# The tail of a fused attention and feed-forward block in another order

## The reference

```python
x = x + attention(layernorm(x))      # 16 heads of 128, rotary q and k, causal window of 128
x = x + ffn(layernorm(x))            # 256 -> 1024 -> 256

# attention: softmax(where(valid, q k^T / sqrt(128), min)) v, heads joined, times wo
# ffn:
w1q, w2q = ternary(w1), ternary(w2)  # round(w / mean|w|) clipped to -1, 0, 1
h = gelu(x @ w1q.T + b1)             # exact gelu
y = h @ w2q.T + b2
```

## Time and profile before

| | us |
|---|---|
| median of 3 runs | 354.56 |
| lowest and highest | 353.38, 354.79 |
| the profiled execution | 352.97 |
| its span, from first to last instruction | 351.2 |
| PE busy | 337.4 (96%) |
| DVE busy | 271.0 (77%) |
| POOL busy | 223.8 (64%) |
| ACT busy | 205.6 (59%) |

### The profile page before, as it was taken

The page is one execution under the profiler, slowest core; times in us unless marked ns, Lnnn a source line. Parts: engine busy times, 40 slices in busy tenths (PEclk is TensorE's granted clock), DMA queues, the critical chain, the costliest instruction groups (busy, mean ns, idle before and its releaser), DMA issues.

```text
span 351.2 us, 6925 instructions
## 1 busy us (share of the span) xinstructions
PE 337.4 (96%) x2410; PEld 312.5 (89%) x2410; DVE 271.0 (77%) x607; ACT 205.6 (59%) x626; POOL 223.8 (64%) x182
## 2 busy tenths in 40 slices
PE   6987999999999999999999999999999999999896
PEld 6876879999999999999999999999999999878886
DVE  4885886778777887799889887887778777868581
ACT  2335775776775556655665566556665566375180
POOL 2327888767677668889898877777777566411300
PEclk9999999999999999999999999999999999999999
DMA  6935565543333333333333333333322231000001
GB/s 206 242 89 153 146 180 152 125 103 87 82 83 88 90 91 90 92 89 82 77 87 83 86 82 83 89 91 91 90 63 60 63 90 32 0 3 0 32 30 60
DMA packets 29025, 31.25 MB, mean 89 GB/s; under 512 B 3392, under 2 KB 20288, under 8 KB 28992
## 3 DMA queue, kind: packets, MB, share of 16 engines
q1 hardware_dynamic: 28992, 30.82, 34.3%
HBM read 12.98 MB, written 1.05 MB: 40 GB/s over the span
## 4 chain that ended last, share of the span: by engine, by line
PE 81%; DVE 8%; DMA 4%; POOL 2%; ACT 2%; issue 1%; SPq 0%; DVEq 0%; POOLq 0%
PE PR L393 23%; PE OT L472 13%; PE VO L410 12%; PE SC L445 11%; PE VO L427 10%; PE PT L456 4%; DMA swapped<-by_sin 3%; PE PR L500 2%; PE SC L500 2%; PE VO L519 1%; POOL turn L970 1%; DVE stats L708 1%; PE SC L519 1%; DVE gT_lo L825 1%; DVE xnorm L721 1%
## 5 line engine op out<-in xcount | busy, mean ns | idle before, releaser
L975 POOL TENSOR_TENSOR gT_lo<-turn,gT_hi 128x512 fp32r<-128x512 f32 x62 | 82.0, 1323 | 45.7 <-ACT gT_hi L605 45.4
L970 POOL TENSOR_TENSOR turn<-turn,swapped 128x512 f32<-128x512 f32 x62 | 80.2, 1293 | 24.9 <-DMA swapped<-by_sin 24.8
L610 ACT ACTIVATE probs<-SC,negmax 128x128 f32<-128x128 f32 x128 | 45.8, 363 | 75.5 <-DVE negmax L772 75.5
L783 DVE TENSOR_TENSOR probsT<-PT,mask_sb 128x512 f32<-128x512 f32 x64 | 44.1, 690 | 40.4 <-PE PT L456 40.3
L472 PE MATMUL OT<-probsT,v_sb 128*128 128x128 f32 x450 | 60.2, 276 | 1.3 <-DVE gT_lo L790 1.3
L472 PEld LDWEIGHTS OT<-probsT,v_sb 128*128 128x128 f32 x450 | 55.2, 192 | 2.3 <-DVE probsT L783 2.1
L617 ACT ACTIVATE probs<-probs,rinv 128x128 f32<-128x128 f32 x128 | 44.5, 394 | 19.1 <-DVE rinv L777 19.1
L393 PE MATMUL PR<-xT_hi,qk_lo 128*128 128x512 f32 x128 | 50.7, 396 | 1.4 <-DVE xT_lo L729 1.4
L393 PE MATMUL PR<-xT_hi,qk_hi 128*128 128x512 f32 x128 | 50.5, 394 | 0.0
L393 PE MATMUL PR<-xT_lo,qk_hi 128*128 128x512 f32 x128 | 50.3, 393 | 0.0
L445 PE MATMUL SC<-gT_hi,gT_lo 128*128 128x256 f32 (+1 forms) x128 | 41.2, 322 | 1.4 <-POOL gT_lo L975 1.3
(11 more groups left out here) (118 smaller groups left out, 836.2 us busy)
## 6 DMA issues: line engine op xcount, KB each, us to landing
swapped<-by_sin SPq DMA_DIRECT2D x128, 128.0 KB, 2.3
qk_raw<-in_wq SPq DMA_DIRECT2D x16, 128.0 KB, 2.6
qk_raw<-in_wk SPq DMA_DIRECT2D x16, 128.0 KB, 2.7
v_raw<-in_wv SPq DMA_DIRECT2D x8, 256.0 KB, 3.0
o_raw<-in_wo SPq DMA_DIRECT2D x8, 256.0 KB, 3.0
xres<-in_x SPq DMA_DIRECT2D x4, 256.0 KB, 3.3
w_raw<-in_w1t SPq DMA_DIRECT2D x4, 256.0 KB, 3.1
w_raw<-in_w2t SPq DMA_DIRECT2D x4, 256.0 KB, 3.0
```

Of the source, the lines that this page charges most:

```text
L610: nc.scalar.activation(probs[n % 2][:, i], SC[n % 2][:, i * 256 + P:(i + 1) * 256], ACT.Exp, bias=negmax[:, n % 2, i:i + 1], accum_out=row ...
L783: tt(probsT[:], PT[:, 0:256].rearrange("p (i q) -> p i q", i=2).unsqueeze(2).broadcast_to([P, 2, 2, P]), mask_sb[:].unsqueeze(1).broadcast ...
L970: tt(turn[m % 4][:], turn[m % 4][:], swapped[m % 2][:], ALU.add).then_inc(rot_done, 1)
L975: tt(rot_lo(head, c % 2)[:, half_of(c)], turn[m % 4][:], rot_hi(head, c % 2)[:, half_of(c)].bitcast(F32), ALU.subtract).then_inc(rotlo_don ...
```

## The change

No instruction is added or taken away, but two casts go to another engine, and the order of several changes.

- ScalarE makes the high halves 4 and 6 too, which VectorE made before. ScalarE's list in the first half is then ghi 1, 3, 4 and 5 behind their gelus, and 6 and 7 behind gelu(7).
- VectorE's tail: `add_out(31)` and `glo(4)` ahead of the four statistics of the second half, `glo(5)` ahead of the moments, `glo(6)` and `glo(7)` ahead of `normalise(1, 1)`.
- VectorE at step 62: `ot_lo(60)` first, `moments(1, 0)` behind `mask_pt(61)`, `normalise(1, 0)` behind `inverse_sum(62)`. At step 63: `xt_lo(1, 0)` ahead of `inverse_sum(63)`.
- TensorE at step 63: `project_out(27)` ahead of the transposes of the first half. ScalarE there: `exps(63)` ahead of the casts of these transposes.
- `ffn2(3)` waits for all sixteen low halves and then finishes tile 6 before it begins tile 7; before, it went over f and did both tiles for each.

```diff
--- before.py
+++ after.py
@@ -245,6 +245,10 @@
             d = (w1_sb, w2_sb)[k][:].rearrange("p a b -> p (a b)")[:, i * 512:(i + 1) * 512]
             return w, d
 
+
+        GHI_ACT = [1, 3, 4, 5, 6, 7] + list(range(NF + 1, 2 * NF, 2))
+        GHI_DVE = [k for k in range(2 * NF) if k not in GHI_ACT]
+
         hb = [PR[0], PR[1], SC[0], SC[1]]
         yb = [VO[0], VO[1], SC[0], SC[1], VO[0], VO[1], PT, OT]
         xt_banks = {(0, 0): SC, (0, 1): SC, (1, 0): PR, (1, 1): [PT, OT]}
@@ -502,6 +506,12 @@
                                   start=(kd == 0 and p_ == 0), stop=(kd == KD - 1 and p_ == 1))
                 last.then_inc(h_done, 1)
 
+            def product(t, f):
+                for p_, gt in enumerate((gT_lo, gT_hi)):
+                    last = mm(yb[t][:, 0:256], gt[:, f, t * P:(t + 1) * P], w2_sb[:, f],
+                              start=(f == 0 and p_ == 0), stop=(f == NF - 1 and p_ == 1))
+                return last
+
             def ffn2(g):
                 tiles = (2 * g, 2 * g + 1)
                 if g == 0:
@@ -511,13 +521,19 @@
                     pe.wait_ge(fin_done, 2)
                 if g == 3:
                     pe.wait_ge(xt_lo_done, 4 * KD)
+                if g == 3:
+
+                    pe.wait_ge(glo_done, 2 * NF)
+                    for t in tiles:
+                        for f in range(NF):
+                            last = product(t, f)
+                        last.then_inc(y_done, 1)
+                    return
                 for f in range(NF):
                     if g % 2 == 0 or f == NF - 1:
                         pe.wait_ge(glo_done, (g // 2) * NF + f + 1)
                     for t in tiles:
-                        for p_, gt in enumerate((gT_lo, gT_hi)):
-                            last = mm(yb[t][:, 0:256], gt[:, f, t * P:(t + 1) * P], w2_sb[:, f],
-                                      start=(f == 0 and p_ == 0), stop=(f == NF - 1 and p_ == 1))
+                        last = product(t, f)
                         if f == NF - 1:
                             last.then_inc(y_done, 1)
 
@@ -545,10 +561,11 @@
                     transpose_probs(n - 1)
                 if n + 4 < CHUNKS:
                     project(n + 4)
+                if n > 0:
+                    fill(n)
                 if n == STEPS - 1:
                     transpose_x(1, 0)
                 if n > 0:
-                    fill(n)
                     weigh_v(n - 1)
             ffn1(0)
             ffn1(1)
@@ -658,10 +675,9 @@
                 p, s = n // 8, n % 8
                 if n >= 2:
                     ot_hi(n - 2)
+                exps(n)
                 if n == STEPS - 1:
                     xt_hi(1, 0)
-                exps(n)
-                if n == STEPS - 1:
                     ot_hi(n - 1)
                     nc.scalar.preload_act_table(ACT.Gelu)
                 if n > 0:
@@ -690,9 +706,11 @@
                 gelu(k)
                 if k == 1:
                     ot_hi(STEPS - 1)
-                if k % 2 == 1:
+                if k in GHI_ACT and k not in (6, 7):
                     ghi(k)
                 if k == NF - 1:
+                    ghi(6)
+                    ghi(7)
                     xt_hi(1, 1)
 
 
@@ -821,7 +839,8 @@
 
             def glo(k):
                 hs = slice((k // NF) * HALF, (k // NF + 1) * HALF)
-                dve.wait_ge(ghi_done[k % 2], k // 2 + 1)
+                by = GHI_ACT if k in GHI_ACT else GHI_DVE
+                dve.wait_ge(ghi_done[1 if k in GHI_ACT else 0], by.index(k) + 1)
                 tt(gT_lo[:, k % NF, hs], hb[k % 4][:], gT_hi[:, k % NF, hs].bitcast(F32),
                    ALU.subtract).then_inc(glo_done, 1)
 
@@ -867,8 +886,7 @@
                     add_out(4 * PAIRS - 3)
                     tile_stats(1, 2)
                     tile_stats(1, 3)
-                    moments(1, 0)
-                if n == STEPS - 1:
+                if n >= STEPS - 2:
                     ot_lo(n - 2)
                 if turned_first(n):
                     mask_pt(n - 1)
@@ -877,16 +895,20 @@
                 merge(n)
                 if n > 0 and not turned_first(n):
                     mask_pt(n - 1)
-                if 1 < n < STEPS - 1:
+                if n == STEPS - 2:
+                    moments(1, 0)
+                if 1 < n < STEPS - 2:
                     ot_lo(n - 2)
                 if n == 0:
                     times_sin(3)
                     times_cos(3)
+                if n + 4 < CHUNKS:
+                    times_sin(n + 4)
+                if n == STEPS - 1:
+                    xt_lo(1, 0)
+                inverse_sum(n)
                 if n == STEPS - 2:
                     normalise(1, 0)
-                if n + 4 < CHUNKS:
-                    times_sin(n + 4)
-                inverse_sum(n)
                 if n + 4 < CHUNKS:
                     times_cos(n + 4)
                 if n <= LP + 4:
@@ -906,7 +928,6 @@
                 i = (n - BELOW_AT - 1) // 2
                 if n > BELOW_AT and (n - BELOW_AT) % 2 == 1 and i < PIECES:
                     ternary(i)
-            xt_lo(1, 0)
             add_out(4 * PAIRS - 5)
             ot_lo(STEPS - 2)
             mask_pt(STEPS - 1)
@@ -918,19 +939,15 @@
             ghi(2)
             glo(2)
             glo(3)
-            tile_stats(1, 4)
-            tile_stats(1, 5)
             add_out(4 * PAIRS - 1)
-            tile_stats(1, 6)
-            tile_stats(1, 7)
+            glo(4)
+            for t in range(4, NT):
+                tile_stats(1, t)
+            glo(5)
             moments(1, 1)
-            ghi(4)
-            glo(4)
-            normalise(1, 1)
-            glo(5)
-            ghi(6)
             glo(6)
             glo(7)
+            normalise(1, 1)
             xt_lo(1, 1)
             for t in range(4):
                 finish(t)
```

## The result

The changed kernel takes 351.45 us as a median of 8 runs (351.02 to 355.15), the kernel before 354.59 in the same series; the ratio is 0.9928, 95% interval 0.9901 to 0.9955, so 1.6 to 3.5 us less. A second series of it gave 0.9949 (0.9922 to 0.9976). I had forecast 352.8 (ratio 0.9950), lowest 351.7: the direction and the mechanism hold, while the first median lies 0.25 us under my range of 351.7 to 354.4.

The account below looks back on a forecast made before the run. TensorE, busy 96% of the span, was taken as the bound, so only gaps between its matmuls could go: +0.43 - 2.10 - 0.10 = -1.77 us, from 354.56 to 352.8; range 351.7 to 354.4.

Parts of the forecast that it names:

- The stall of 2.10: In ffn2(0), TensorE waits for VectorE's low halves; the new tail order and casts remove it all, minus 2.10 us.
- Rival B: In the tail, the wait moves to ScalarE with its six casts; gain falls to 1.1, 353.5 us; chance 0.14.
- The front, +0.43: Steps 62 and 63: normalise(1,0) now waits for rstd, so ffn1(0) starts 0.43 us late, a loss.
- Rival A: At steps 62 and 63, the reordering costs nothing, covered by earlier TensorE work; sum -2.20, 352.4 us; chance 0.12.
- The end, -0.10: Last two tiles: finished tile by tile, the last finish on VectorE comes 0.10 us earlier.
- Rival C: TensorE idle at the front drops the granted clock to 1.2 of 2.4 GHz; slower, 356.3 us; chance 0.06.
- a clock below 1.00: Granted clock of TensorE in the new profile; a fall below 1.00 would show the forecast wrong.

Follow-up runs that it names:

- e2: Kernel before with only VectorE's new tail order and high halves 4 and 6 on ScalarE; merge(61) to end 52.44 us (before 54.50), ratio 0.9929.
- e1: Kernel before with only the new order of steps 62 and 63; merge(61) to end 54.83 us (before 54.50), ratio 1.0027.
- e4: Changed kernel with steps 62 and 63 put back in the old order; merge(61) to end 52.17 us (changed kernel 52.47).
- e3: Kernel before with only ffn2(3) changed, tile 6 finished before tile 7 begins; merge(61) to end 54.23 us (before 54.50), ratio 0.9995.
- e10: Changed kernel profiled once more, no edit; merge(61) to end 52.50 us (first profile 52.47).
- e7: Changed kernel with moments(1,0) back right behind the statistics; merge(61) to end 51.65 us (changed kernel 52.47), ratio 0.9897.
- e9: e7 with TensorE's transposes and ScalarE's casts at step 63 in the old order; merge(61) to end 51.69 us, ratio 0.9908.

## Why the prediction was right, term by term

- **The stall of 2.10** in ffn2(0): gone, 2.09 by the trace and in e2 alone (5.93 to 3.84). Rival B, that ScalarE takes its place, is out: glo(6) waited 0.17 us for ScalarE (I had 0.3), and glo(7) ended 0.67 before TensorE wanted it.
- **The front, +0.43**: the mechanism as given, the size +0.32 (0.33 alone in e1). normalise moved by 1.21 (forecast 1.24), merge(63) by 0.64 (0.66); most of the rest is at the exponentials: the first cast starts 0.70 us after exps(63) begins, not 0.8. Rival A, a front for nothing, is out by e1 and e4.
- **The end, -0.10**: the last finish came 0.11 earlier against TensorE's last matmul, as forecast. I had not priced the last store, whose issue no longer follows another: this is worth 0.13 to 0.16 more (e3).
- **Rival C**, the clock: nothing of it in the tail, where TensorE's longest idle in step 63 was 0.95 us and the clock stayed 1.00. I had named a clock below 1.00 as a sign of being wrong, and the first profile has a mean of 0.990; but both falls are in its head, ahead of the change, and e10 has 0.999. My evidence against this rival was weaker than I took it for (last section).
- The sum by trace is -2.03 for -1.77, the front's 0.11 and the store's 0.13 making the difference. The first medians moved by more (-3.14); the ratio of the second series, 0.9949, is 1.8 us. In the two profiles of the changed kernel the stretch from merge(61) repeats to 0.1 us, while the heads differ with the same instructions; so I put what goes beyond 2.03 down to the heads, which only the profiled executions show.

What stays open: why fewer executions of the changed kernel had a low mean clock. Of the runs of before in the three later series, 25 of 65 had a mean clock under 0.997, of the changed kernel 1 of 8 and 2 of 12. No run tells chance from a cause here.

## What to carry to other kernels

Where TensorE is 96% busy, look for the one stretch in which it is not, and read the order of the engine that it waits for: an engine that is never idle can be the cause, by doing first what is wanted last. Where another engine must turn a small result round (here 0.25 us to start and 1.04 to run), put its producer as early as its inputs allow and its consumer as late as can be: the change did the second, undid the first, and lost 0.8 us that e7 gives back. Compare traces from a point ahead of the edits when the head of an execution varies by more than the effect.

## What the runs showed of the hardware that I had not expected

The granted clock does fall in this kernel, in its head, after idle times that I had taken for harmless. In the profile after, TensorE waited 1.99 us before this matmul and 1.76 before the other:

```profile
18.75 0.47 PE L397 MATMUL PR<-xT_hi,qk_lo 128*128 128x512 f32 x1 [1.99 <-DVE xT_lo L747]
```

```profile
49.89 0.38 PE L449 MATMUL SC<-gT_hi,gT_lo 128*128 128x256 f32 x1 [1.76 <-POOL gT_lo L992]
```

Behind each the clock is at the lower level, 0.50, 1.2 of 2.4 GHz (windows; the column after the engines is the clock):

```profile
16.00:24.00 8.00, 6.01 (x27) 4.96 (x26) 6.45 (x13) 3.19 (x8) 1.28 (x1) 0.79 0.33 84
20.00:21.00 1.00, 1.00 (x5) 0.74 (x3) 0.73 (x2) 0.00 (x0) 0.00 (x0) 0.50 0.00 0
...
48.00:56.00 8.00, 6.24 (x33) 5.41 (x32) 5.14 (x12) 4.96 (x19) 6.85 (x6) 0.79 0.48 134
51.00:52.00 1.00, 1.00 (x6) 0.90 (x5) 0.64 (x2) 0.89 (x2) 0.27 (x2) 0.50 0.92 169
```

Two stretches of eight microseconds thus had a mean of 0.79; by my estimate each lost about 8 x 0.21 = 1.7 us. That fits e10, the same kernel without the falls, whose merge(61) comes 3.63 us earlier. In the profile before the same first wait was 1.38 us, and the clock stayed 1.00 (the row at 16 to 20 on which I argued against rival C):

```profile
18.21 0.47 PE L393 MATMUL PR<-xT_hi,qk_lo 128*128 128x512 f32 x1 [1.38 <-DVE xT_lo L729]
```

It would be wrong to read a limit between 1.38 and 1.76 out of this. In e10 the first wait was 1.94 us, and in e9 there was one of 1.85, and behind both the clock stayed 1.00 (e10, then e9):

```profile
18.71 0.47 PE L397 MATMUL PR<-xT_hi,qk_lo 128*128 128x512 f32 x1 [1.94 <-DVE xT_lo L747]
...
16.00:24.00 8.00, 5.86 (x37) 4.79 (x35) 7.30 (x15) 3.41 (x9) 1.28 (x1) 1.00 0.36 88
```

```profile
48.62 0.39 PE L448 MATMUL SC<-gT_hi,gT_lo 128*128 128x256 f32 x1 [1.85 <-POOL gT_lo L988]
...
48.00:56.00 8.00, 7.27 (x46) 6.23 (x47) 6.63 (x17) 5.38 (x18) 7.27 (x7) 1.00 0.58 164
```

So the clock fell behind a wait of 1.76 us in one execution and not behind 1.85 or 1.94 in two others: the length of a single wait does not decide it, and what does stays open. One row at 1.00 after a wait, as I used it against rival C, therefore excludes little. What speaks against it is the tail of the profile after itself, where the clock was 1.00 throughout, here over the waits of step 63:

```profile
310.00:320.00 10.00, 8.67 (x54) 6.94 (x54) 7.70 (x17) 6.08 (x15) 2.79 (x4) 1.00 0.01 2
```
